# A fused attention and expert kernel on one core: two loads, one group of key turns and ACT's transfers moved in the first pair, and a new order of the ending

## The chip, the cores and the metric

The kernel runs on one core of a Trainium2 chip. Its engines work in parallel, each through its own list of instructions in order, and are held together by semaphores: PE (matrix multiply), DVE (vector), ACT (scalar), POOL (GpSimd) and SP, which here only issues transfers. Transfers run on 16 DMA engines that all queues share. The metric is the device time of one execution in microseconds (us); less is better. The kernel before took 330.53 us, the median of three runs from 329.59 to 330.92.

## The reference, cut to what matters

The input is x of 8 batches of 64 rows by 512, and a context of 8 batches of 1601 rows by 512. Three blocks follow one another, each added to x:

```
x = x + cross(layernorm(x), context)     # scores over 1601 keys, softmax, values
x = x + attn(layernorm(x))               # 16 heads of 32, a sigmoid in place of the softmax, gates
x = x + experts(layernorm(x))            # each row goes to the one of 8 experts with the top logit
# attn:    k, q = l2norm(xn @ Wk), l2norm(xn @ Wq)
#          res = sigmoid((q k^T - 0.295) * 15);  out = ((res * gate_q * gate_k) @ v) @ Wo + bo
# experts: sel = argmax(x @ gate_w.T);  out += (xs @ w_up.T * silu(xs @ w_gate.T)) @ w_down.T
```

The gates are dot products of q and k with the short vectors gq and gk. Everything is 32-bit float.

## The kernel before, in words

**Pairs.** Two batches make a pair of 128 rows (a row per partition), so there are four pairs, numbered 0 to 3 (`_L` is 3, `_B` is 2). Pair 0 is written out, pairs 1 and 2 are a loop, pair 3 is written out again. For each pair PE computes the scores of the pair against its own 1601 keys in 13 units (`score`, lines 1304 to 1348), ACT takes the exponentials, PE turns them (`turn_numerators`) and weighs the context with them (`weigh`), in four chunks of keys. The self attention of pair p - 1 runs between the score units of pair p, as steps with names: "sum", "on", "y" (cross attention's value product), "stats", "norm", "a2" (row statistics, normalization and its turn), "q", "k", "v", "graw", "fold" (products and gates), "kT", "turn" (turned keys and queries), "align0", "align1" (the scores of the heads), "bd" (DVE writes the sigmoid's values in diagonal blocks), "gT", "col" (collapse), "o" (output product), "h", "route", "rank" (top expert and the row's place in the expert's list).

**Keys.** The scores need the keys turned. Part of them PE turns through PSUM (`turn_keys`, lines 1269 to 1277; ACT and DVE move the result, `move_keys`, line 342). The rest is read from the context a second time in a layout that DVE can turn in place: `load_split` (line 364) issues transfers of 512-byte pieces in parts 0 to 3, and `turn_split` (line 868) turns them on DVE into the ring CT_sb. For pair 1 SP issues the lower half of parts 0 and 1, and ACT the upper half, in `upper_first` (line 762), between its copies. Part 2 of pair 1 is issued by SP once DVE has turned part 0 of pair 1.

**Weights in the first pair.** SP's list is in order. From line 439 it reads: attention weights awq and awk, context chunk 1, split part 0 (lower), wv, split part 1 (lower), awv, awo, and then split part 2. POOL waits for awq and awk (lines 565 and 566) and multiplies them, 512 columns at a time, by gq and gk (line 575, eight times). Behind the second multiplication, still in POOL's order, stands `pair_bias(0)`, which copies `ccur`, a bias per row. DVE's `shift(0)` (line 891: the maximum of the scores and this bias) needs `ccur`, and ACT's exponentials need the shift. DVE sums the products of POOL (`gate_sums`, line 1081), two buffers in turn.

**The ending.** Behind pair 3's weighing stands the list `ENDING` (line 88) and then `LATE` (line 93). All engines walk the same two lists, and each picks out its own part of every step. Entries with `_L` are steps of pair 3's self attention, the others steps of the wide expert tiles 0 to 3 (64 rows of each of two experts): "get" (POOL gathers the rows), "xT" (turn), "up0" to "up3" (gate and up products, 4 matmuls each), "act" (ACT's tanh, then two operations of DVE), "hT" (turn), "down" (8 matmuls, and DVE's addition of the result to the rows). The rows that don't fit in the wide tiles go into two narrow tiles 4 and 5, whose rows are known only after pair 3's "rank": DVE makes the choice (`choose(_L)`), PE finds the rows (`find_tokens`), POOL gathers them, and a loop of rounds (one round here) computes them, behind `LATE`. After `ENDING` DVE first counts how many rounds there are (lines 1172 to 1176), then makes the choice, then finds the rows, and then does the first "act" of `LATE`. POOL scatters the finished rows; tiles of `LATE_WIDE` are scattered in the loop of rounds, the others in `ENDING`, and `stored` counts the scatters for the last wait.

## Time and profile before

| | us |
|---|---|
| median of three runs | 330.53 |
| the profiled execution | 324.69 |
| its span, first to last instruction | 323.0 |
| PE busy | 294.6 (91%) |
| DVE busy | 165.2 (51%) |
| ACT busy | 87.9 (27%) |
| POOL busy | 79.4 (25%) |
| mean granted TensorE clock | 0.975 of full |

The profiled execution was shorter than the median of the timed runs. The span ends with the scatter of the last narrow tile, issued at 318.62 us. The chain of work that ended last is of no use here: it holds that scatter alone (0.3% of the span). So the order of time and the idle time in front of instructions have to be read instead. In such a row the columns are: start, duration, engine, line, operation, destination<-source, shape, count, and in brackets the idle time of the engine just before and what ended it. Neighbouring instructions of one kind are merged into one row.

### The profile page before, as it was taken

Reading aid. Unit: us, or ns where it says so; the run is one execution under the profiler, and the core shown is the slowest. Engines: PE = TensorE matmul, PEld = TensorE weight load, DVE = VectorE, ACT = ScalarE, POOL = GpSimd, SP = SyncE. Lnnn points to the kernel's source line nnn. Section 1 sums busy time; section 2 is a strip of 40 time slices with the busy share of each in tenths; the row PEclk is TensorE's granted clock in tenths of the full one; section 3 lists DMA queues with packets and bytes.
Section 4 is the critical chain, followed back from the end, with each engine's and each line's share of the span. In section 5 each row is a group of like instructions: output and inputs, shape, how many; then the busy total and the mean of one; then the engine's idle time right before and its main releaser. Section 6 shows DMA issues by size and latency. Waiting matters only on the chain. (4 is left out here: it accounts for less than half of the span.)

```text
span 323.0 us, 4958 instructions
## 1 busy us (share of the span) xinstructions
PE 294.6 (91%) x1628; PEld 143.3 (44%) x1628; DVE 165.2 (51%) x381; ACT 87.9 (27%) x209; POOL 79.4 (25%) x87
## 2 busy tenths in 40 slices
PE   5899998999679999999999999998998899898992
PEld 4689544633223554333465433455533244442330
DVE  3305382373086767448594638657551434735341
ACT  2133211444001436310264510143411114411210
POOL 5300003328112600022440021262111435103202
PEclk9799998999959999999999999999999999999998
DMA  7999999999996999899999399999215995152300
GB/s 238 375 296 286 231 315 318 289 232 275 227 386 200 213 270 223 168 306 386 234 229 338 81 207 380 309 298 360 90 67 179 422 411 225 42 213 78 143 13 36
DMA packets 67541, 77.41 MB, mean 240 GB/s; under 512 B 3220, under 2 KB 46260, under 8 KB 66497
## 3 DMA queue, kind: packets, MB, share of 16 engines
q1 hardware_dynamic: 60656, 69.76, 76.6%
q0 software_dynamic: 1552, 4.78, 4.2%
q10 hardware_dynamic: 5312, 2.62, 3.7%
q8 instruction: 11, 0.18, 0.2%
q14 instruction: 10, 0.07, 0.1%
HBM read 74.00 MB, written 3.67 MB: 240 GB/s over the span
## 5 line engine op out<-in xcount | busy, mean ns | idle before, releaser
L874 DVE STREAM_TRANSPOSE CT_sb<-FF_sb 128x1024 f32<-128x1024 f32 (+1 forms) x56 | 50.7, 952 | 22.0 <-DMA FF_sb<-ctx 20.8
L1385 PE MATMUL ST<-CTX_sb,PR_sb 128*64 128x512 f32 (+1 forms) x208 | 48.2, 600 | 1.1 <-ACT PR_sb L361 1.1
L1347 PE MATMUL SC<-CT_sb,QC_sb 128*64 128x512 f32 x112 | 29.8, 650 | 4.9 <-DVE CT_sb L874 4.9
L1230 PE MATMUL A<-AW_sb,normT_sb 128*128 128x512 f32 x64 | 29.5, 604 | 0.1
L1385 PEld LDWEIGHTS ST<-CTX_sb,PR_sb 128*64 128x64 f32 (+1 forms) x208 | 13.9, 136 | 23.2 <-issue 22.3
L1230 PEld LDWEIGHTS A<-AW_sb,normT_sb 128*128 128x128 f32 x64 | 11.5, 189 | 15.7 <-issue 11.9
L1253 PE MATMUL A<-AW_sb,WQK_sb 128*128 128x256 f32 x64 | 15.9, 412 | 1.5 <-DMA WQK_sb<-wq 1.5
L546 POOL TENSOR_TENSOR rn_sb<-ss_sb,nhalf_sb 128x16 f32<-128x16 f32 x4 | 11.7, 2917 | 22.3 <-DVE ss_sb L948 22.3
L575 POOL TENSOR_TENSOR sq_sb<-AW_sb,rowv_sb 128x512 f32<-128x512 f32 x4 | 5.1, 1273 | 45.9 <-DMA AW_sb<-awk 35.2
L1347 PEld LDWEIGHTS SC<-CT_sb,QC_sb 128*64 128x64 f32 x112 | 7.3, 144 | 20.2 <-issue 11.0
L1230 PE MATMUL A<-AO_sb,rawT_sb 128*128 128x512 f32 x32 | 14.8, 605 | 1.2 <-DVE rawT_sb L987 1.2
L1327 PE MATMUL SC<-CT_sb,QC_sb 128*64 128x256 f32 x112 | 15.7, 418 | 0.0
L1253 PEld LDWEIGHTS A<-AW_sb,WQK_sb 128*128 128x128 f32 x64 | 13.1, 208 | 3.9 <-DMA WQK_sb<-wq 1.8
L1230 PE MATMUL A<-WV_sb,rawT_sb 128*128 128x512 f32 x32 | 14.7, 602 | 0.0
L693 ACT COPY QC_sb<-QK_sb 32x128 f32 (+1 forms) x48 | 14.2, 296 | 1.1
L1286 PE MATMUL A<-AO_sb,WQK_sb 128*128 128x128 f32 (+1 forms) x64 | 14.5, 382 | 0.0
L714 ACT COPY rawT_sb<-A 128x512 f32<-128x512 f32 x4 | 2.3, 586 | 42.8 <-PE A L1223 34.3
L549 POOL TENSOR_TENSOR rn_sb<-ss_sb,nhalf_sb 128x16 f32<-128x16 f32 x4 | 11.6, 2903 | 6.8 <-DVE ss_sb L955 6.8
L540 POOL TENSOR_TENSOR rstd_sb<-rstd_sb,halves_sb 128x3 f32<-128x3 f32 x4 | 3.5, 877 | 39.2 <-DVE rstd_sb L933 39.2
L558 POOL TENSOR_TENSOR rstd_sb<-rstd_sb,nhalf_sb 128x1 f32<-128x1 f32 x4 | 2.2, 562 | 39.5 <-DVE rstd_sb L995 39.5
L701 ACT ACTIVATE PR_sb<-SC,mx_sb 128x512 f32<-128x512 f32 x12 | 8.1, 684 | 12.9 <-DVE mx_sb L898 12.9
L889 DVE TENSOR_REDUCE mx_sb<-SC 128x1 f32<-128x512 f32 x12 | 8.2, 681 | 6.4 <-PE SC L1327 6.3
(261 smaller groups left out, 482.4 us busy)
## 6 DMA issues: line engine op xcount, KB each, us to landing
CTX_sb<-ctx SPq DMA_DIRECT2D x24, 1024.0 KB, 11.7
FF_sb<-ctx SPq DMA_DIRECT2D x48, 256.0 KB, 6.9
FF_sb<-ctx SPq DMA_DIRECT2D x52, 128.0 KB, 6.1
CTX_sb<-wgu SPq DMA_DIRECT2D x4, 1024.0 KB, 13.0
CTX_sb<-wdn SPq DMA_DIRECT2D x5, 512.0 KB, 16.4
FF_sb<-ctx ACTq DMA_DIRECT2D x8, 256.0 KB, 12.1
FF_sb<-wgu SPq DMA_DIRECT2D x2, 1024.0 KB, 7.6
rows<-XR_sb SPq DMA_DIRECT2D x3, 512.0 KB, 7.3
```

The lines of the kernel that those rows point to most:

```text
L546: g.tensor_tensor(rn[:, 0:HEADS], ss[:, 0:HEADS], nhalf[:, 0:HEADS], ALU.pow).then_inc(s["powq"], 1)
L549: g.tensor_tensor(rn[:, HEADS:], ss[:, HEADS:], nhalf[:, HEADS:], ALU.pow).then_inc(s["powk"], 1)
L693: a.copy(qcurP[m * Q:(m + 1) * Q, j, :], qk[j * Q:(j + 1) * Q, m, bass.ds(p * P, P)]).then_inc(s["qcurP_made"], 1)
L701: a.activation(prow[:, keys], chunk_scores[c], ACT.Exp, bias=mx[:, NCH + 2:NCH + 3], scale=scale, accum_out=esum[:, c:c + 1]).then_inc(s[" ...
L874: v.transpose(ring[:, c, :, to:to + n * Q].rearrange("p k (b r) -> p k b r", r=Q), split[:, :, at:at + n, c * Q:(c + 1) * Q]).then_inc(s[" ...
L889: link(v.tensor_reduce(mx[:, c:c + 1], chunk_scores[c], AX.X, ALU.max))
L1230: last = t_.matmul(bank, left[:, c, :], right[:, c, :], start=(c == 0), stop=(c == DC - 1))
L1253: last = t_.matmul(AB[m % 2][:, 0:2 * P], wq[:, c, m * P:(m + 1) * P], xnT[:, c, 2 * P * half:2 * P * (half + 1)], start=(c == 0), stop=(c ...
L1286: last = t_.matmul(AB[m % 2][:, n], wkT[:, c, m * P:(m + 1) * P], qpT[:, c, n], start=(c == 0), stop=(c == DC - 1))
L1327: last = t_.matmul(SC[q, at:at + GT * P], queries(p, own)[:, i, q], ring[:, i, k, at:at + GT * P], start=(i == 0), stop=(i == DC - 1))
L1347: last = t_.matmul(SC[q, ch * D:(ch + 1) * D], queries(p, own)[:, c, q], ring[:, c, k, :], start=(c == 0), stop=(c == DC - 1))
L1385: last = t_.matmul(ST[q, :], probs[0:w, t, q], ctxb[0:w, k, t, :], start=(t == 0), stop=(t == KT - 1))
```

## The change

It has four parts. In SP's list awq and awk go behind the lower half of split part 0, and wv behind the lower half of part 1. On ACT both `upper_first` go behind the copies of the turned keys, the copy of `crow` comes earlier, and the copy of `call` stands between the two. On DVE the four `turn_split` of pair 1's first keys go in front of the gate sums and of the move of the numerators. The ending gets a new order, with tile 1's act, hT and down in `LATE`; DVE's choice goes in front of the counting of the rounds.

```diff
-ENDING = ((0, "get"), (1, "get"), (_L, "sum"), (0, "xT"), (_L, "on"), (1, "xT"), (_L, "y"), (0, "up0"), (0, "up1"), (0, "up2"), (0, "up3"),
-          (_L, "stats"), (_L, "norm"), (2, "get"), (3, "get"), (_L, "a2"), (1, "up0"), (0, "act"), (_L, "q"), (_L, "graw"), (0, "hT"),
-          (_L, "k"), (_L, "fold"), (_L, "v"), (0, "down"), (2, "xT"), (_L, "kT"), (_L, "turn"), (1, "up1"), (1, "up2"),
-          (_L, "align0"), (_L, "align1"), (1, "up3"), (2, "up0"), (_L, "bd"), (_L, "gT"), (1, "act"), (_L, "col"), (3, "xT"),
-          (_L, "o"), (1, "hT"), (_L, "hnorm"), (_L, "h"), (1, "down"), (_L, "route"), (2, "up1"), (2, "up2"), (_L, "rank"), (2, "up3"))
-LATE = ((2, "act"), (3, "up0"), (3, "up1"), (2, "hT"), (3, "up2"), (3, "up3"), (3, "act"), (2, "down"), (3, "hT"), (3, "down"))
+ENDING = ((0, "get"), (1, "get"), (_L, "sum"), (0, "xT"), (_L, "on"), (_L, "y"), (0, "up0"), (0, "up1"), (0, "up2"), (0, "up3"),
+          (_L, "stats"), (_L, "norm"), (2, "get"), (3, "get"), (_L, "a2"), (0, "act"), (1, "xT"), (_L, "q"), (_L, "graw"), (0, "hT"),
+          (_L, "k"), (_L, "fold"), (_L, "v"), (_L, "kT"), (_L, "turn"), (1, "up0"), (1, "up1"), (_L, "align0"), (_L, "align1"),
+          (0, "down"), (_L, "bd"), (_L, "gT"), (_L, "col"), (2, "xT"), (_L, "o"), (1, "up2"), (_L, "hnorm"), (_L, "h"), (1, "up3"),
+          (_L, "route"), (2, "up0"), (2, "up1"), (_L, "rank"), (2, "up2"))
+LATE = ((1, "act"), (2, "up3"), (1, "hT"), (3, "xT"), (2, "act"), (1, "down"), (3, "up0"), (2, "hT"), (3, "up1"), (3, "up2"),
+        (2, "down"), (3, "up3"), (3, "act"), (3, "hT"), (3, "down"))
-LATE_WIDE = (2, 3)
+LATE_WIDE = (1, 2, 3)
...
             sp.wait_ge(s["qp_made"], 2 * DC)
-            load_weight(awq, "awq", "aq_in")
-            load_weight(awk, "awk", "ak_in")
             load_chunk(0, 1)
             sp.wait_ge(s["keysT_made"], split_turned(0, FIRST.keys(1, 3)))
             load_split(sp, 1, 0, LOWER)
-            load_weight(wv, "wv", "wv_in")
+            load_weight(awq, "awq", "aq_in")
+            load_weight(awk, "awk", "ak_in")
             sp.wait_ge(s["keysT_made"], split_turned(0, FIRST.keys(0, 3)))
             load_split(sp, 1, 1, LOWER)
+            load_weight(wv, "wv", "wv_in")
             load_weight(awv, "awv", "av_in")
...
-            for turn in FIRST.turns[2:6]:
+            for turn in FIRST.turns[2:5]:
+                move_keys(act, a.copy, 0, 0, turn)
+            act.wait_ge(s["c_made"], 1)
+            a.copy(crow, AB[1][:, :]).then_inc(s["c_moved"], 1)
+            for turn in FIRST.turns[5:]:
                 move_keys(act, a.copy, 0, 0, turn)
             upper_first(0, FIRST.keys(1, 3), 0)
-            move_keys(act, a.copy, 0, 0, FIRST.turns[6])
-            act.wait_ge(s["c_made"], 1)
-            a.copy(crow, AB[1][:, :]).then_inc(s["c_moved"], 1)
-            upper_first(0, FIRST.keys(0, 3), 1)
             act.wait_ge(s["c_made"], 2)
             a.copy(call[:], AB[1][:, 0:PAIRS + E]).then_inc(s["c_moved"], 1)
+            upper_first(0, FIRST.keys(0, 3), 1)
             exponentials(0)
...
-            gate_sums(0, 2)
-            move_numerators(dve, v.tensor_copy, 0, 1)
             for c in range(DC):
                 turn_split(1, 1, c)
-            gate_sums(2, 4)
+            move_numerators(dve, v.tensor_copy, 0, 1)
+            gate_sums(0, 4)
             move_numerators(dve, v.tensor_copy, 0, 3)
...
+            dve.wait_ge(s["slot_made"], PAIRS)
+            choose(_L)
             link(v.tensor_tensor(cnt[:, 2:2 + E], A1[:, E:2 * E], filled[:], ALU.add))
...
             v.tensor_scalar(rounds[0:1, 0:1], cnt[0:1, 1:2], 1.0, None, ALU.add).then_inc(s["rounds_made"], 1)
...
-            dve.wait_ge(s["slot_made"], PAIRS)
-            choose(_L)
             dve.wait_ge(s["tok_made"], 1)
             find_rows(link)
```

## Rows read from the trace of the kernel before

**Rows 1.** The page: PE's busy time, and the DMA share in 40 slices.

```profile
PE 294.6 (91%) x1628; PEld 143.3 (44%) x1628; DVE 165.2 (51%) x381; ACT 87.9 (27%) x209; POOL 79.4 (25%) x87
DMA  7999999999996999899999399999215995152300
```

**Rows 2.** Windows: stretch, length, busy by engine, then PEclk, DMA share, GB/s.

```profile
48.00:50.00 2.00, 2.00 (x14) 1.23 (x16) 0.71 (x1) 0.00 (x0) 0.42 (x1) 1.00 1.05 397
52.00:54.00 2.00, 1.61 (x14) 1.09 (x14) 0.00 (x0) 0.82 (x2) 0.07 (x1) 1.00 1.10 320
78.00:84.00 6.00, 6.00 (x23) 2.25 (x20) 0.00 (x0) 1.09 (x2) 4.06 (x4) 1.00 1.23 216
54.00:58.00 4.00, 4.00 (x23) 2.66 (x24) 0.00 (x0) 0.00 (x0) 0.00 (x0) 0.57 1.21 254
```

**Rows 3.** DMA issues: the load of awk, with KB and us to landing.

```profile
AW_sb<-awk SPq DMA_DIRECT2D x1, 1024.0 KB, 9.6
```

**Rows 4.** Order of time, the first pair, from gates to first weighing.

```profile
49.58 1.27 POOL L575 TENSOR_TENSOR sq_sb<-AW_sb,rowv_sb 128x512 f32<-128x512 f32 x1 [35.20 <-DMA AW_sb<-awk]
...
52.39 1.08 PE L1327 MATMUL SC<-CT_sb,QK_sb 128*64 128x256 f32 x8 [1.53 <-ACT CT_sb L351]
...
59.93 0.69 ACT L701 ACTIVATE PR_sb<-SC,mx_sb 128x512 f32<-128x512 f32 x1 [1.70 <-DVE mx_sb L898]
...
62.22 0.49 ACT L681 COPY QK_sb<-A 128x384 f32<-128x384 f32 x1
...
64.49 0.59 ACT L361 COPY PR_sb<-TR 128x512 f32<-128x512 f32 x1
...
65.13 3.65 PE L1385 MATMUL ST<-CTX_sb,PR_sb 128*64 128x512 f32 x16 [0.24 <-ACT PR_sb L361]
```

**Rows 5.** Order of time: part 2 of pair 1 issued, and waited for.

```profile
70.25 12.51 SPq L370 DMA_DIRECT2D FF_sb<-ctx  x8
...
89.21 3.50 DVE L874 STREAM_TRANSPOSE CT_sb<-FF_sb 128x1024 f32<-128x1024 f32 x3 [11.51 <-DMA FF_sb<-ctx]
90.51 5.15 PE L1347 MATMUL SC<-CT_sb,QC_sb 128*64 128x512 f32 x12 [4.90 <-DVE CT_sb L874]
...
96.28 0.66 PE L1223 MATMUL A<-ident_sb,a_sb 128*128 128x128 f32 x4 [0.62 <-DVE a_sb L936]
```

**Rows 6.** Windows: the ending, from the last weighing to the narrow tiles.

```profile
245.64:303.26 57.62, 52.40 (x264) 22.74 (x265) 26.35 (x69) 13.02 (x27) 16.95 (x13) 1.00 0.58 224
```

**Rows 7.** Order of time, the ending, around "a2" and "q".

```profile
256.95 2.67 DVE L943 TENSOR_SCALAR normT_sb<-rawT_sb,vec_sb 128x128 f32<-128x128 f32 x4 [1.30 <-ACT rawT_sb L714]
257.63 1.08 PE L1589 MATMUL SC<-CTX_sb,QK_sb 128*64 128x512 f32 x4 [1.34 <-DMA CTX_sb<-wdn]
```

**Rows 8.** Order of time, the ending, from tile 0's "down" to "col".

```profile
270.09 1.94 PE L1610 MATMUL SC<-FF_sb,QK_sb 128*64 128x512 f32 x8
...
272.07 0.69 DVE L1159 TENSOR_TENSOR CT_sb<-SC,CT_sb 128x512 f32<-128x512 f32 x1 [3.52 <-PE SC L1610]
...
275.70 1.95 PE L1437 MATMUL A<-WQK_sb,rawT_sb 128*64 128x256 f32 x16 [0.34 <-issue]
...
278.30 1.78 DVE L981 TENSOR_SCALAR WQK_sb<-res_sb 64x512 f32<-64x512 f32 x4
...
280.14 1.08 PE L1452 MATMUL A<-WQK_sb,vs_sb 128*32 128x128 f32 x32 [0.19 <-DVE WQK_sb L981]
```

**Rows 9.** Order of time, behind "rank", and around tile 3's last "up".

```profile
293.23 0.16 DVE L1172 TENSOR_TENSOR cnt_sb<-A,filled_sb 128x8 f32<-128x8 f32 x1
...
294.54 0.20 PE L1564 MATMUL A<-token_sb,CT_sb 128*128 128x1 f16 x2 [0.96 <-DVE CT_sb L1036]
...
295.52 0.42 DVE L1155 SCALAR_TENSOR_TENSOR QK_sb<-QK_sb,TR 128x256 f32<-128x256 f32 x1
...
298.25 0.59 PE L1589 MATMUL SC<-WV_sb,QK_sb 128*64 128x512 f32 x1
...
299.76 0.42 DVE L1155 SCALAR_TENSOR_TENSOR QK_sb<-QK_sb,SC 128x256 f32<-128x256 f32 x1
```

More of the change, by code:

```diff
@@ L262, in x_bank, with stored @@
             return A1 if f == NT - 1 else TR[0]
-        def stored(r):
-            return 16 * ((NW - len(LATE_WIDE)) // 2 + (len(LATE_WIDE) + NN) // 2 * (r + 1))
+        def stored(i, r):
+            wide = sum(f % 2 == i for f in range(NW) if f not in LATE_WIDE)
+            late = sum(f % 2 == i for f in LATE_WIDE + tuple(range(NW, NT)))
+            return 16 * (wide + late * (r + 1))
         def tile_number(f, r):
@@ L646, in _ @@
                 for i in range(2):
-                    pool.wait_ge(s_stored[i], stored(r))
+                    pool.wait_ge(s_stored[i], stored(i, r))
                 settle(pool)
@@ L1171, in _, with find_rows @@
             link, n = linker("round_chain", 0)
+            def find_rows(link):
+                link(v.tensor_reduce(tok[:, 2, :], token_bank.rearrange("p (i f) -> p f i", i=PAIRS), AX.X, ALU.add))
+                v.tensor_scalar(idxg[:], tok[:, 2, :], -1.0, 0.0, ALU.add, ALU.max).then_inc(s["idxg_made"], 1)
+            dve.wait_ge(s["slot_made"], PAIRS)
+            choose(_L)
             link(v.tensor_tensor(cnt[:, 2:2 + E], A1[:, E:2 * E], filled[:], ALU.add))
@@ L1176, in _ @@
             v.tensor_scalar(rounds[0:1, 0:1], cnt[0:1, 1:2], 1.0, None, ALU.add).then_inc(s["rounds_made"], 1)
-            def find_rows(link):
-                link(v.tensor_reduce(tok[:, 2, :], token_bank.rearrange("p (i f) -> p f i", i=PAIRS), AX.X, ALU.add))
-                v.tensor_scalar(idxg[:], tok[:, 2, :], -1.0, 0.0, ALU.add, ALU.max).then_inc(s["idxg_made"], 1)
-            dve.wait_ge(s["slot_made"], PAIRS)
-            choose(_L)
             dve.wait_ge(s["tok_made"], 1)
@@ L1210, in _ @@
                 for i in range(2):
-                    dve.wait_ge(s_stored[i], stored(r))
+                    dve.wait_ge(s_stored[i], stored(i, r))
                 assert n[0] == ROUND_LINKS
```

## The prediction

> **What bounds the kernel now.** I read the page first. PE is busy for 294.6 us of the 323.0, and the DMA share is at 9 tenths without a break over the first slices, then it loosens [rows 1]. So PE's stream sets the time wherever it has work, and the first hundred microseconds are the place where transfers could set it. The chain that ended last shows only the last scatter, so I went through PE's idle times in order of time. There are two kinds of them. In the start PE waits 1.53 us for an ACT copy at 52.39 [rows 4], and 4.90 us ahead of 90.51 for keys that DVE could not turn, because DVE itself waited 11.51 us for split part 2 of pair 1 [rows 5]. That second wait ends with a transfer. In the ending, from 245.64 to 303.26, PE is busy 52.40 of 57.62 us, which leaves 5.2 us of idle time in some nine pieces [rows 6]. PE does the same matmuls after the change, so it can win at most these pieces, and it loses what new ones open.
>
> **The start: where the first shift goes.** The windows give the DMA's speeds: pieces of 2 KB alone go at 397 GB/s, pieces of 512 bytes from one queue at 216, 2 KB from SP beside 512 bytes from ACT at 320, and 512 bytes from both at 254 [rows 2]. In SP's list chunk 1 (2.1 MB) now has the place of awq and awk (2.1 MB), so it lands when awk did: POOL's first gate product, released by awk, starts at 49.58, and awk took 9.6 us from its issue [rows 3, 4]. Then comes the lower half of part 0, 1.05 MB at 216 GB/s: 4.9 us, to 54.3. ACT's upper half is now issued only from about 50 us. Then awq and awk, 2.1 MB, beside ACT's small pieces. If the DMA engines take turns piece by piece, SP gets four fifths of 320 GB/s, or 256: 8.2 us, and awk lands at 62.5. The bounds: with nothing beside it 2.1 MB take 5.3 us (59.6); with all of ACT's 1.05 MB ahead of it at 216 GB/s 67.3. I take 62.5, since the 320 GB/s were measured with both kinds in flight.
>
> The Trainium skill ("DMA: Bandwidth & Descriptors", section "Queues, rings and completion order") says that each DMA engine takes turns between the queues at the grain of a packet of several descriptors. With packets of like counts that is my piece-by-piece share; with ACT's packets shorter, awk would land up to 3 us sooner.
>
> POOL's order is gates 0 and 1 and then the copy of `ccur`, and DVE's shift needs `ccur`. So the shift, which waited for ACT's copy of `call` before, now waits for awk: two products of 1.27 us [rows 4] and three or four short instructions of some 0.2 us each (the like of 0.16 in rows 9), 0.7 us. The exponentials start at 62.5 + 2.5 + 0.7 = 65.7 instead of 59.93. ACT then goes on as before: 2.3 us to its copy at 62.22, two such copies of 0.49, and the numerators' copy of 0.59 [rows 4]. In the old order these lay under PE's products of queries; now they are behind each other, and the first weighing starts at 65.7 + 2.3 + 1.0 + 0.6 = 69.6 instead of 65.13, 4.5 us late. ACT's issues behind its copies do remove the 1.53 us at 52.39, and the half clock behind it (granted clock 0.57 from 54 to 58 [rows 2]), but PE only reaches the numerators sooner, at about 61, and waits there longer. After such a wait it runs at the low clock of 1.2 GHz for some microseconds: behind the 4.90 us of rows 5, 12 matmuls took 5.15 us where four take 1.08 at 2.4 GHz [rows 7], 1.9 us too much. I take 2.4 for the longer wait. PE is 6.9 us late when it comes to pair 1's scores.
>
> What covers this: PE waited 4.90 us there anyway, the 1.9 us of low clock go with that wait, and another 0.62 us of idle time stands ahead of 96.28 [rows 5]. Together 7.4 us, so 6.9 us cost nothing, with 0.5 us to spare. If awk lands at 67.3, 4.8 us later, 4.3 us are left over.
>
> **The start: pair 1's keys.** DVE turns them right behind the shift: 4 turns of about 1.2 us (three took 3.50 [rows 5]). From 66.1 they end near 70.9, about where they ended before (SP issued part 2 at 70.25, which waits for them [rows 5]). So this move wins nothing: the transfer they wait for and the late shift hold them. Nor would an earlier issue help, for the same bytes stand ahead of part 2 in the queues and the DMA is never idle there. DVE's move of numerators 1 is now behind the turns, at 71.6; PE needs it behind the first weighing, at 69.6 + 3.65 + the low clock, later than 75. The gate sums come later too (end near 83, before the pair's sum needs DVE at about 84), and POOL's clearing and added row end near 88, ahead of the 92 us at which DVE wants them. These cost nothing with some microseconds of cover; on the low side they can't gain, since part 2 holds everything.
>
> Part 2's landing itself may move. Some 1000 more of ACT's small pieces now run beside 2 KB pieces rather than beside other small ones. At 320 against 397 GB/s such a piece costs 2.8 ns, at 254 against 216 it costs 1.7 ns: 1.2 us more in all. Bounds -1 (the order could as well spare the slow passage from small to large pieces) to +1.2; I take +0.8. All that comes later in pair 1 shifts by it.
>
> **The ending.** I walked PE's new list with the durations of before (product 3.5, "up" 0.87, "down" 1.87, turn 0.5 from start to start).
> - Behind "on" PE has no xT of tile 1 left to do: idle +0.3. Tile 1's "up0" no longer stands ahead of "q", so the 1.34 us wait for tile 1's weights goes [rows 7]. In its place PE waits for normT: 0.7 us until its first quarter is there, and 0.9 us because DVE's four operations take 2.67 us [rows 7] beside POOL's gathers and addition. Together +0.3.
> - From "align0" DVE's order is: two scalings, then **tile 0's addition**, then "bd". The addition waits for "down" of tile 0, which PE does behind "align1". Before: "align" at 275.70, "bd" at 278.30, "col" at 280.14 [rows 8]. Now, counted from "align0": "down" starts at +1.75, its result is added from +1.75 + 1.98 = +3.7 (270.09 to 272.07 [rows 8]) for 0.69, "bd" runs from +4.4 for 1.78, and "col" can start at +6.25. PE's fill is "down" 1.87 and "gT" 0.5, which end at +4.15. A hole of 2.1 us instead of 0.19. Without the addition in front "bd" would end at +4.45.
> - The waits of 0.34 [rows 8] and of about 0.6 ahead of "h" go, and that ahead of "o" shrinks by 0.2, since other steps fill them: -1.1.
> - The choice in front of the counting: about 0.9 us of DVE's counting (from 293.23 to PE's 294.54, less the choice itself and the signal) leave the way to PE's wait of 0.96 us [rows 9]. With less fill ahead, 0.4 us are left: -0.6.
> - Tile 1's "act" now stands on DVE behind choice, counting and finding, 2.4 us in all (293.23 to 295.94 less the wait inside [rows 9]). PE has 0.15 + 0.87 us to do meanwhile: a hole of 1.1 us ahead of "hT" of tile 1.
> - At the end of `LATE` "down" of tile 2 stood between tile 3's last "up" and its "hT". Now it stands ahead of that "up", and nothing is between. From the last matmul of "up" (298.25) to the end of "act" on DVE (300.18) it takes 1.93 us [rows 9], of which 0.45 is the matmul's own pace: a hole of 1.5 us.
>
> The pieces sum to 0.3 + 0.3 + 1.9 - 1.1 - 0.6 + 1.1 + 1.5 = +3.4. Walking the starts instead I reach the narrow tiles at 305.9 against 303.26, +2.6, since a few changes of kind between steps disappear. I take +2.7. The narrow rows are gathered some 3 us sooner, but PE had no idle time left ahead of 303.26, so that hides nothing new. Bounds: -1.9 if neither hole of DVE's order opens, +3.4 if all do.
>
> On normT: the Trainium skill ("SBUF — State Buffer", section "Who interferes with whom") says that VectorE in its two-port mode and GpSimd lock each other out for whole instructions. The 2.67 us agree. If POOL's addition fell clear of the four operations in the new order, 0.9 us of the hole at "q" would go and the sum be 0.9 lower; POOL's steps shift with DVE's, so I leave it.
>
> **The sum.** The profiled execution took 324.69 us (span 323.0 and 1.7 around it). 324.69 + 0 + 0.8 + 2.7 = 328.2. The median of the timed runs was 330.53, 5.8 us above the profiled one; I take the same difference of 3.5 us there: 334.0.
>
> **Rivals.**
> *The ending's new order pays (faster).* The mechanism is in the ending: the waits on tile 1's weights (1.34), on the choice (0.6 of 0.96) and of the short ones (1.1) go, and the two holes of DVE's order and the last "hT" don't open, because PE reaches "down" of tile 0 or tile 3's "up" late enough. Then it is -1.9, with part 2 at +0.2: 328.8. It decides if the hole ahead of "col" stays under 0.3 us and that ahead of tile 3's "hT" under 0.5. For it: the old list has real waits there. Against: the old list had a "down" as fill in the last place, the new one has nothing.
> *awk lands late, beyond the cover (slower still).* Should ACT's transfers take more of the DMA, 4 us come on top: 338. Against: the share of 320 GB/s measured with both in flight.
> *They cancel.* Only one of the DVE holes opens, or part 2 lands 1 us sooner: 331.5, no change that can be told.
> That the change doesn't do what it says is in the forecast itself: the first keys are turned no earlier, as the shift comes later.
>
> **Chances.** A measurement of this kernel tells a change from none at about 0.5%, 1.65 us. Forecast 0.53, awk late 0.12, cancelled 0.17, faster 0.18. So slower 0.65, same 0.17, faster 0.18. The range goes from 328.8 (the first rival; half of its chance lies below) to 337.8, near the second; the forecast's own is 332 to 336.
>
> **What would show it.** POOL's first line 575 row near 62.6, and the first exponential near 65.7; PE idle there for some 4 to 5 us; no idle piece over 1 us ahead of the scores of pair 1 near 90; the PE row of line 1452 ("col") behind a wait of 2 us for line 981; a wait of 1.5 us ahead of tile 3's "hT". I am wrong if `ccur` is there before 60 us, or if the ending's idle sum is under 5 us.

## The result, and the profile after

The changed kernel took 334.24 us (median of four runs, 331.1 to 335.0), the kernel before 330.06 beside it. The ratio, here and below, is taken over the fast runs alone and so needn't be that of the medians: 1.032, 95% interval 1.020 to 1.044. In a second comparison, with 30 runs of before and 7 of the changed kernel, the medians were 328.91 and 332.42, ratio 1.011 (1.003 to 1.019). Both say slower, by 1 and by 3%; the size can't be had closer, since the kernel before, measured against itself, gave a ratio of 1.021 (below). The forecast was 334.0, +3.5 us, ratio 1.0106.

The changed kernel's page: the same work on PE, DVE, ACT and POOL as in [rows 1], but a span of 332.2 us, 9.2 more. PEclk, the granted clock in tenths of full, drops in slices 8 to 10, in and behind the long wait of the start, and once more in slice 35, in the ending.

```profile
PE 294.8 (89%) x1628; PEld 143.7 (43%) x1628; DVE 165.3 (50%) x381; ACT 87.5 (26%) x209; POOL 79.4 (24%) x87
PEclk9999999757999999999999999999999999799997
DMA  6999999999996998899999699999026992524000
```

Its order of time at the start. This answers [rows 4] and [rows 5]: awk ends the wait at 67.07, where 62.6 was forecast; POOL needs two products and the copy of `ccur`; the first exponential follows at 70.22, not 65.7; PE waits 12.30 us for it. Part 2 is issued at 75.10 and DVE starts on its last pieces at 92.32.

```profile
67.07 1.26 POOL L578 TENSOR_TENSOR sq_sb<-AW_sb,rowv_sb 128x512 f32<-128x512 f32 x1 [52.89 <-DMA AW_sb<-awk]
68.29 1.25 POOL L578 TENSOR_TENSOR kh_sb<-AW_sb,rowv_sb 128x512 f32<-128x512 f32 x1
69.49 0.18 POOL L532 COPY ccur_sb<-call_sb 128x1 f32<-128x1 f32 x1
...
70.22 0.69 ACT L704 ACTIVATE PR_sb<-SC,mx_sb 128x512 f32<-128x512 f32 x1 [18.97 <-DVE mx_sb L902]
70.38 4.62 DVE L878 STREAM_TRANSPOSE CT_sb<-FF_sb 128x1024 f32<-128x1024 f32 x4
71.05 1.97 PE L1359 MATMUL TR<-ident_sb,PR_sb 128*128 128x128 f32 x8 [12.30 <-ACT PR_sb L704]
...
75.10 10.08 SPq L373 DMA_DIRECT2D FF_sb<-ctx  x8
...
92.32 3.50 DVE L878 STREAM_TRANSPOSE CT_sb<-FF_sb 128x1024 f32<-128x1024 f32 x3 [3.12 <-DMA FF_sb<-ctx]
...
99.84 0.66 PE L1226 MATMUL A<-ident_sb,a_sb 128*128 128x128 f32 x4
```

PE's wait of 4.90 us in [rows 5] is gone, and still the a2 turn of pair 0 comes at 99.84 instead of 96.28. In the chain of waits (start, length, what) this stretch is now awk, the exponentials, then PE's work up to the product "y" at 92.48 and DVE's steps behind it; the wait for part 2 isn't in it. The waits for the next pairs' split parts are.

```profile
51.08 15.83 DMA AW_sb<-awk
70.22 2.41 ACT PR_sb L704 x8
73.93 6.37 PE ST L1388 x16
...
92.48 3.65 PE A L1233 x8
...
138.38 8.07 DMA FF_sb<-ctx
...
192.28 8.04 DMA FF_sb<-ctx
```

The ending, in the order of time. Against [rows 7]: "q" waits twice for DVE's quarters of normT. Against [rows 8]: "col" (line 1455) waits 1.89 us, since DVE adds tile 0 first (line 1162, 281.53) and then makes the four products. Against [rows 9]: the wait on the choice is 0.17, and two new waits of 0.86 and 1.49 stand ahead of the hT of tiles 1 and 3.

```profile
262.44 2.66 DVE L947 TENSOR_SCALAR normT_sb<-rawT_sb,vec_sb 128x128 f32<-128x128 f32 x4 [1.30 <-ACT rawT_sb L717]
262.84 1.12 PE L1233 MATMUL A<-AW_sb,normT_sb 128*128 128x512 f32 x2 [0.62 <-DVE normT_sb L947]
...
264.64 1.55 PE L1233 MATMUL A<-AW_sb,normT_sb 128*128 128x512 f32 x3 [0.68 <-DVE normT_sb L947]
...
281.53 0.69 DVE L1162 TENSOR_TENSOR CT_sb<-SC,CT_sb 128x512 f32<-128x512 f32 x1 [1.02 <-PE SC L1613]
282.14 1.77 DVE L985 TENSOR_SCALAR WQK_sb<-res_sb 64x512 f32<-64x512 f32 x4
283.96 1.73 PE L1455 MATMUL A<-WQK_sb,vs_sb 128*32 128x128 f32 x32 [1.89 <-DVE WQK_sb L985]
...
297.68 0.20 PE L1567 MATMUL A<-token_sb,CT_sb 128*128 128x1 f16 x2 [0.17 <-DVE CT_sb L1040]
...
299.74 0.41 PE L1601 MATMUL ST<-ident_sb,QK_sb 128*128 128x128 f32 x2 [0.86 <-DVE QK_sb L1158]
...
309.71 0.41 PE L1601 MATMUL ST<-ident_sb,QK_sb 128*128 128x128 f32 x2 [1.49 <-DVE QK_sb L1158]
```

The 9.19 us between the two traces lie in three places, counted from one instruction to its counterpart: 3.56 up to pair 0's a2 turn (96.28 to 99.84), 2.26 from there to the last weighing product (148.77 against 151.03), where not a line is changed, and 3.37 in the ending (58.70 to 62.07). The tail is equal. So one comparison of two traces puts a quarter of the loss into untouched code, and this is what the experiments had to explain.

### The profile page after: what moved, and what is told of

Same layout as the page of the kernel before. It is cut to its first block, busy times and chain, and to the rows that moved or that the text cites. A ratio compares the mean times of both kernels' runs of the same rounds, so it can differ in the third digit from the quotient of the medians.

```text
span 332.2 us, 4959 instructions
## 1 busy us (share of the span) xinstructions
PE 294.8 (89%) x1628; PEld 143.7 (43%) x1628; DVE 165.3 (50%) x381; ACT 87.5 (26%) x209; POOL 79.4 (24%) x87
## 4 chain that ended last, share of the span: by engine, by line
PE 60%; DVE 13%; DMA 12%; SPq 5%; issue 4%; ACT 3%; POOL 1%; DVEq 0%; POOLq 0%; ACTq 0%
PE A L1233 15%; PE ST L1388 8%; DVE CT_sb L878 5%; DMA FF_sb<-ctx 5%; DMA AW_sb<-awk 5%; PE A L1256 4%; SPq L373 4%; PE SC L1330 4%; PE SC L1592 3%; PE SC L1613 3%; PE TR L1233 3%; PE A L1289 3%; PE A L1226 3%; PE A L1440 2%; DMA WQK_sb<-wq 2%
## 5 line engine op out<-in xcount | busy, mean ns | idle before, releaser
L1388 PE MATMUL ST<-CTX_sb,PR_sb 128*64 128x512 f32 (+1 forms) x208 | 50.9, 628 | 1.8 <-ACT PR_sb L364 1.8
L1350 PE MATMUL SC<-CT_sb,QC_sb 128*64 128x512 f32 x112 | 27.2, 603 | 0.0
L1388 PEld LDWEIGHTS ST<-CTX_sb,PR_sb 128*64 128x64 f32 (+1 forms) x208 | 14.6, 143 | 26.0 <-issue 24.3
L578 POOL TENSOR_TENSOR sq_sb<-AW_sb,rowv_sb 128x512 f32<-128x512 f32 x4 | 5.1, 1265 | 64.0 <-DMA AW_sb<-awk 52.9
L1359 PE MATMUL TR<-ident_sb,PR_sb 128*128 128x128 f32 (+1 forms) x52 | 9.0, 304 | 12.3 <-ACT PR_sb L704 12.3
L1359 PEld LDWEIGHTS TR<-ident_sb,PR_sb 128*128 128x128 f32 (+1 forms) x52 | 6.6, 153 | 20.2 <-ACT PR_sb L704 13.6
L1256 PE MATMUL A<-AW_sb,WQK_sb 128*128 128x256 f32 x64 | 14.2, 381 | 1.1 <-DMA WQK_sb<-wq 1.1
L1330 PE MATMUL SC<-CT_sb,QC_sb 128*64 128x256 f32 x112 | 14.3, 388 | 0.0
L1256 PEld LDWEIGHTS A<-AW_sb,WQK_sb 128*128 128x128 f32 x64 | 12.0, 190 | 2.9 <-DMA WQK_sb<-wq 1.4
```

Of the source, the lines that this page charges most:

```text
L1256: last = t_.matmul(AB[m % 2][:, 0:2 * P], wq[:, c, m * P:(m + 1) * P], xnT[:, c, 2 * P * half:2 * P * (half + 1)], start=(c == 0), stop=(c ...
L1330: last = t_.matmul(SC[q, at:at + GT * P], queries(p, own)[:, i, q], ring[:, i, k, at:at + GT * P], start=(i == 0), stop=(i == DC - 1))
L1350: last = t_.matmul(SC[q, ch * D:(ch + 1) * D], queries(p, own)[:, c, q], ring[:, c, k, :], start=(c == 0), stop=(c == DC - 1))
L1359: last = t_.transpose(TR[c % 2][0:w, (t - lo) * P:(t - lo + 1) * P], prow[:, t * P:t * P + w], ident[:, :])
L1388: last = t_.matmul(ST[q, :], probs[0:w, t, q], ctxb[0:w, k, t, :], start=(t == 0), stop=(t == KT - 1))
```

## The experiments

**What one trace is worth: the kernel before, again.**

> The kernel before, unchanged, profiled and timed once more, to see what a second execution of the same program differs by. Theory A (all of the 9.2 us between the two profiles is the change): part 2 of pair 1 lands near 89.1 again, its 256 KB pieces 1.25 us apart, and the span is 323 +- 1. Theory B (some 2 to 3 us of the 9.2 us are the DMA's speed in that execution, since the pieces of part 2 came 1.33 us apart in the changed kernel's profile and the loop of pairs lost 0.9 us per pair there): the pieces come 1.3 to 1.35 us apart in some executions of this kernel too, and the span is 325 to 328.

Six runs had the median 334.83 (330.5 to 336.4), beside 328.47 over eleven runs of the same program (325.9 to 336.9): a ratio of 1.021 (1.015 to 1.027) between a kernel and itself. Five of the six lie within 2 us (334.5 to 336.4), which doesn't look like independent draws from the wide spread. The intervals take them as independent and are then too narrow: here a ratio up to some 1.02 proves nothing by itself. In its order of time the a2 turn comes at 99.27, where the changed kernel has 99.84.

```profile
92.19 3.50 DVE L874 STREAM_TRANSPOSE CT_sb<-FF_sb 128x1024 f32<-128x1024 f32 x3 [13.32 <-DMA FF_sb<-ctx]
...
93.50 4.53 PE L1347 MATMUL SC<-CT_sb,QC_sb 128*64 128x512 f32 x12 [5.86 <-DVE CT_sb L874]
...
99.27 0.65 PE L1223 MATMUL A<-ident_sb,a_sb 128*128 128x128 f32 x4 [1.24 <-DVE a_sb L936]
```

So the rival that puts the difference into the spread between executions holds here: DVE's last turns of part 2 come 3 us later than in [rows 5], and the a2 turn with them, in an unchanged kernel. The first profile of before was one of its fastest executions.

**The change in halves: its start alone, twice, and its ending alone.** start_only is the changed kernel with the old lists and the old place of the choice; ending_only is the reverse.

```diff
 # start_only, start_again: the changed kernel with
-ENDING, LATE, LATE_WIDE = the new ones;   choose(_L) ahead of the counting
+ENDING, LATE, LATE_WIDE = the old ones;   choose(_L) behind the counting
 # ending_only: the kernel before with the new ones
```

> The changed kernel with the ending of before (both lists, the late tiles, and choice behind counting). If the parts add up, PE waits some 10 to 12 us for the first exponential, the a2 turn of pair 0 is 3 to 3.6 us later than before, and the whole is +1 to +3.5 us against before (1.003 to 1.011). By my forecast's sum the start costs 0.8 us (1.002).

> The kernel before with the new ending alone. Forecast of the mechanism: a hole of 1.9 to 2.1 us ahead of col and 1.5 us ahead of the last hT of the wide tiles, the way from the last weighing to the narrow tiles is 60.5 to 61 us instead of 57.6, the whole +2.7 to +3.8 us (1.008 to 1.0115). The rival, that the removed waits pay for the holes, says -1.9 to +0.5 us.

> The changed start with the ending of before, as start_only, once more, for its second trace and its median. Theory 1 (the late shift is a bound of its own): pair 0's a2 turn comes 32 to 33 us behind the landing of awk and more than 7.2 us behind that of part 2; the wait for awk costs 0.4 to 3 us, the more the faster part 2 lands, so the median is 1 to 2 us above that of before, ratio 1.004, and the lowest runs of before (322) are not reached. Rival (the cover of 7.4 us holds, and only part 2 counts): a2 exactly 7.2 us behind part 2, ratio 1.00 and the same lowest runs.

start_only: 331.39 us (325.3 to 338.4), ratio 1.000 (0.992 to 1.008). start_again: 329.38 over twelve runs (322.8 to 336.4) beside 328.14 (322.5 to 335.3), no interval. ending_only: 330.89, ratio 1.008 (1.002 to 1.014). Beside the 1.021 of a kernel against itself no time here tells one of the halves from nothing; both have to be measured in the order of time. For the start: in start_only DVE has the last pieces at 90.13, 2 us sooner than in the second trace of before, and the a2 turn comes no sooner:

```profile
70.61 1.97 PE L1358 MATMUL TR<-ident_sb,PR_sb 128*128 128x128 f32 x8 [9.42 <-ACT PR_sb L703]
...
90.13 3.50 DVE L877 STREAM_TRANSPOSE CT_sb<-FF_sb 128x1024 f32<-128x1024 f32 x3 [1.36 <-DMA FF_sb<-ctx]
...
99.41 0.66 PE L1225 MATMUL A<-ident_sb,a_sb 128*128 128x128 f32 x4
```

From DVE's first of these turns to the a2 turn it takes 7.07 or 7.08 us in all eleven traces whose first shift doesn't wait for awk, whatever their total. In the four with the changed start it takes 7.52, 9.28, 7.92 and 7.59 (after, start_only, after_again, start_again), and there the a2 turn comes 32.9, 32.9, 32.3 and 33.1 us behind the landing of awk. So there are two bounds, part 2 and the late shift, and in the changed kernel the second is the later one, by 0.4 to 2.2 us, mean 1.0. The rival in start_again, that part 2 alone counts, is refuted by the trace (7.59 and not 7.07); its other half, that the lowest runs stay as low, came true (322.8 and 322.5). In time the start's cost of about 1 us is below what the runs tell.

**The late shift taken away.**

```diff
+            pair_bias(0)
             pool.wait_ge(s["rowv_in"], 16)
             pool.wait_ge(s["aq_in"], 16)
...
-                if n == 2:
-                    pair_bias(0)
```

> The changed kernel with POOL's copy of ccur in front of its waits for awq and awk, so that the first shift does not hang on awk. Theory 1 (the bias behind awk is what costs at the start): PE's 12.3 us wait for the first exponential goes, and the a2 turn of pair 0 comes 3 us earlier, so the whole is 3 us (0.991) faster than the changed kernel. Theory 2 (the landing of part 2 of pair 1 sets it, and it is late because the DMA moved the same bytes more slowly): the 12.3 us wait goes too, but PE waits 8 to 10 us for the keys near 92 instead, and the a2 turn of pair 0 gains under 0.7 us.

336.05 us, one of six runs far out (750.5), no ratio. The order of time shows the exchange: the exponentials start at 62.48 although awk landed only at 70.4, and the 12.30 us of PE's wait become 2.96 there and 5.83 for part 2. Part 2 was slow in this execution, and a2 comes at 102.03, not sooner. DVE's turn of pair 1's first keys, which the change put right behind the shift, starts only at 68.86, behind a wait of 12.36 us for their transfer.

```profile
62.48 0.69 ACT L703 ACTIVATE PR_sb<-SC,mx_sb 128x512 f32<-128x512 f32 x1 [9.62 <-issue]
...
94.96 3.50 DVE L877 STREAM_TRANSPOSE CT_sb<-FF_sb 128x1024 f32<-128x1024 f32 x3 [11.81 <-DMA FF_sb<-ctx]
...
96.26 4.81 PE L1349 MATMUL SC<-CT_sb,QC_sb 128*64 128x512 f32 x12 [5.83 <-DVE CT_sb L877]
...
102.03 0.66 PE L1225 MATMUL A<-ident_sb,a_sb 128*128 128x128 f32 x4 [0.97 <-DVE a_sb L939]
```

**What part 2's landing is worth, in both directions.** In weights_late awv and awo are issued behind it, in more_bytes two more transfers of 1 MB stand ahead of it (their copies are read by nobody).

```diff
 # weights_late
-            load_weight(awv, "awv", "av_in")
-            sp.wait_ge(s["qk_made"], 2 * DC)
-            sp.wait_ge(s["c_made"], 2)
-            load_weight(awo, "awo", "awo_in")
             split_after(1, NEXT.keys(1, 3), 1, 2)
+            (the same four lines)
 # more_bytes
             load_weight(awv, "awv", "av_in")
+            for i in range(2):
+                sp.dma_start(spare[i], A["awk"]).then_inc(s["spare_in"], 16)
```

> The kernel before, with one thing moved on SP: the two weights of the second attention's values and output (awv, awo, 1 MB each as they lie in memory) are issued behind the second split part of pair 1 instead of ahead of it. Theory 1 (the landing of that part sets pair 0's a2 turn, whatever the start does, and it is set by the bytes queued ahead of it): part 2 lands 4 to 6 us earlier (before: 92.1 in the second profile of that kernel, so about 87), the wait of 5.9 us that PE has for it shrinks to under 2 us, pair 0's a2 turn comes at 95 to 96 instead of 99.3 (or at 93 where the pace of the pieces is the fast one), the last weighing and the end come as much earlier, 3 to 4 us, ratio 0.990. Theory 2 (the part is late because it is issued late and its pieces have their own pace of 1.3 us each): it lands at the same time, ratio 1.00. Theory 3 (the two weights then arrive too late for v and o of pair 0): the wait only moves to there, ratio 1.00 with a wait on L1419's awv or on awo.

> The kernel before with two more 1 MB transfers on SP's queue behind awv, from the memory of the chip to a place in it that nothing reads, so two weights' bytes more stand ahead of the second split part of pair 1; nothing else is changed, and no engine waits for them. Theory 1 (what stands in the stream ahead of that part sets pair 0's a2 turn, and a later turn is carried to the end): the part lands about 5 us later (97 instead of 92), the wait of PE for it grows by as much, pair 0's a2 turn comes at 104 to 105 instead of 99 to 100, and the run is 4 to 5 us longer, ratio 1.013. Taken with the run in which two weights were moved behind the part (a2 turn at 93.9, the end where it was), it says whether the start counts in one direction only. Rival (the stream has slack later, so the periods of pairs 1 to 3 take the 5 us back): the a2 turn is as late, but the last weighing comes under 2 us later, ratio 1.005 or less.

more_bytes: 334.64 us beside 328.0, ratio 1.030 (1.019 to 1.041). The a2 turn is at 104.17, 4.9 later than in before_again, and the last one at 265.91 against 261.33 there: next to that trace nothing is given back, and the rival with its slack falls. Of the 6.6 us between the medians (more than the 4 to 5 expected) this explains 4.6 to 4.9. The size rests on single traces: over the six with the old start and the old bytes the a2 turn lies between 96.28 and 102.89 and the last one between 255.63 and 264.91. The direction rests on more: both turns of more_bytes lie behind all of them, and from the issue of part 2 (70.70) to DVE's first turn of it takes 26.4 us, against 19.0 to 22.3 in those six.

```profile
97.09 3.50 DVE L877 STREAM_TRANSPOSE CT_sb<-FF_sb 128x1024 f32<-128x1024 f32 x3 [19.91 <-DMA FF_sb<-ctx]
...
98.39 4.37 PE L1350 MATMUL SC<-CT_sb,QC_sb 128*64 128x512 f32 x12 [14.03 <-DVE CT_sb L877]
...
104.17 0.66 PE L1226 MATMUL A<-ident_sb,a_sb 128*128 128x128 f32 x4 [1.41 <-DVE a_sb L939]
```

weights_late: 328.43 beside 328.91, ratio 1.002 (0.995 to 1.009). The a2 turn is at 93.92, 5.4 earlier than in before_again, more than expected, but the 3 to 4 us expected at the end didn't come: DVE waits 4.02 us for part 3 until 111.09, PE waits 3.82 behind it, and the a2 turn of pair 1 comes at 153.51, where before_again has 153.72.

```profile
86.85 3.50 DVE L874 STREAM_TRANSPOSE CT_sb<-FF_sb 128x1024 f32<-128x1024 f32 x3 [6.38 <-DMA FF_sb<-ctx]
...
93.92 0.65 PE L1223 MATMUL A<-ident_sb,a_sb 128*128 128x128 f32 x4 [2.11 <-DVE a_sb L936]
...
111.09 2.49 DVE L874 STREAM_TRANSPOSE CT_sb<-FF_sb 128x512 f32<-128x512 f32 x4 [4.02 <-DMA FF_sb<-ctx]
...
115.13 2.96 PE L1437 MATMUL A<-WQK_sb,rawT_sb 128*64 128x256 f32 x16 [3.82 <-issue]
```

The stretch from pair 0's a2 turn to pair 1's says it without regard to an execution's pace: 59.6, 61.2 and 60.4 us in the three traces with the two weights late (weights_late, choose_late_w, turn_first; the last two below), 52.9 to 54.5 in the twelve others. So bytes put ahead of part 2 are carried to the end. Moving bytes behind it pays only until the next part, which has the same bytes ahead of it as ever.

**The changed kernel again.**

> The changed kernel with nothing altered, in the same call. If runs of one program differ by up to 2 per cent from execution to execution through the pace of the first 90 us of transfers, as the kernel before did (325.9 to 336.9 over eleven runs), this one comes out at 331 to 337, and its ratio to the kernel before lies between 1.00 and 1.02, not at 1.032 again. Its profile should have the stretch from the last weighing to the last tile's turn at 61 to 62 us and the holes ahead of col (1.9) and of tile 3's hT (1.5), whatever its total; pair 0's a2 turn may lie anywhere from 96 to 100.

332.42 us over seven runs beside 328.91 over thirty: ratio 1.011 (1.003 to 1.019). Time and ratio were as expected, the holes and the stretch too (1.89, 1.49, 60.9). Only the a2 turn, 101.40, lies above the 96 to 100 expected.

**The ending's holes closed one after the other**, on the kernel before with the new ending.

```diff
 # end_col: tile 0's down behind col
-          (0, "down"), (_L, "bd"), (_L, "gT"), (_L, "col"), (2, "xT"), ...
+          (_L, "bd"), (_L, "gT"), (_L, "col"), (0, "down"), (2, "xT"), ...
 # end_both: end_col, and in LATE
-        (2, "down"), (3, "up3"), (3, "act"), (3, "hT"), (3, "down"))
+        (3, "up3"), (3, "act"), (2, "down"), (3, "hT"), (3, "down"))
```

> The kernel before with the new ending (as ending_only), but tile 0's down step is put behind col instead of ahead of bd, so that DVE's addition of that tile (0.69 us) no longer stands ahead of the four block-diagonal products that col waits for. Theory 1 (the hole of 1.9 us ahead of col is that addition with its wait for PE's product, and the clock falls behind the hole): the hole shrinks to under 1.2 us, o runs in 3.7 instead of 4.2 us, and the stretch from the last weighing's last product to the last tile's turn (58.6 in the kernel before, 60.9 in ending_only, 62.1 in after) is 1.0 to 1.6 us shorter than in ending_only: 59.5 to 60. Rival (col waits for the gate mask or for vp, not for the four products): the hole stays and the stretch stays at 60.9.

> As end_col, and in the late part tile 2's down step moves from ahead of tile 3's up3 to between tile 3's activation and its hT, so that 0.9 us of PE's work lies where PE stood for 1.49 us. Theory 1: that hole falls to 0.6 us or less, the stretch is another 0.9 us shorter than in end_col, about 58.8, which is what the kernel before has (58.6): the new order is then worth nothing once its holes are closed. Rival: the activation of tile 3 is now late behind up3, so the hole of 0.86 ahead of tile 1's hT and the one at tile 3 only change places: stretch as in end_col, 59.5 to 60.

Medians 330.60 and 330.61 beside 328.91, ratios 1.003 (0.996 to 1.009) and 1.003 (0.997 to 1.009). The windows from pair 3's a2 turn to the turn of the last narrow tile tell more (length, PE busy, PEclk, DMA share, GB/s). The kernel before, first trace; its second one has 48.22:

```profile
255.63:303.75 48.12, 44.08 (x232) 1.00 0.53 205
```

The changed kernel, first and second trace (ending_only has 50.63, at full clock too):

```profile
261.13:312.94 51.81, 46.07 (x236) 0.97 0.50 195
```

```profile
263.74:314.35 50.61, 44.65 (x236) 1.00 0.52 203
```

end_col and end_both:

```profile
260.91:312.84 51.93, 46.24 (x236) 0.97 0.50 196
```

```profile
262.85:311.62 48.77, 44.53 (x236) 1.00 0.53 205
```

At the full clock the new ending takes 50.6 us and the old one 48.2 in this window: +2.4. Of it 1.9 are idle time (50.6 less 44.7 against 48.1 less 44.1), and 0.5 are the four matmuls of tile 1's "xT" (x236 against x232), which stood ahead of the a2 turn in the old order. From the last weighing on, with them in both, it is 60.9 against 58.6 and 58.7: +2.2. end_both brings the window to 48.77 and the whole stretch to 59.0, 0.3 to 0.5 above the old order and 0.8 to 0.9 above the old order with the same early choice (58.1 and 58.2, below). Neither kernel's time differs from before beyond the interval.

Its two edits together are worth 1.9, and the waits say which of them: nearly all is the second. In end_col the wait ahead of "col" is 0.98 instead of 1.90, but a new one of 0.89 stands ahead of "gT", where "down" had been PE's fill; end_both has 0.99 and 0.88. Their sum is what the one hole was. "col" comes 1.7 us sooner, counted from "align0" (4.4 instead of 6.1), and then PE has "down" still to do, which takes as long. Only a wait of 0.23 ahead of "o" went with it. The second edit took the whole 1.49 us ahead of tile 3's hT away.

```profile
280.43 0.63 PE L1226 MATMUL A<-ident_sb,kh_sb 128*128 128x128 f32 x4 [0.89 <-DVE res_sb L973]
282.05 1.75 PE L1455 MATMUL A<-WQK_sb,vs_sb 128*32 128x128 f32 x32 [0.98 <-DVE WQK_sb L984]
```

**The best part alone, and two candidates.** choose_early is the kernel before with the choice ahead of the count; choose_late_w adds weights_late; turn_first is the changed start with the bias first, the weights late, and the old order with the choice early.

> The kernel before with one small part of the ending's change alone: DVE makes the last pair's choice and the lookup of rows ahead of the five small instructions that count the rounds, as the changed kernel does; the order of steps stays as before. Theory: the wait of 0.96 us that PE has for DVE's pick ahead of the lookup product falls to 0.2 us, as in the changed kernel, and nothing is late behind it, so the stretch from the last pair's a2 turn to the last tile's turn, 48.1 to 48.2 at full clock in three traces, becomes 47.4, ratio 0.998. Rival: tile 2's product fills PE behind it anyway, the count of rounds is late for the tail, and the stretch stays at 48.2.

> choose_early with the two weights issued behind the second split part of pair 1, as in weights_late, as the candidate for a version faster than both kernels. If the two edits are independent: pair 0's a2 turn at 94, the last stretch at 47.4, and the run 0.5 to 1.3 us shorter than the kernel before, ratio 0.997; what the earlier a2 turn brings is expected to be lost again in pair 1, where the next split part comes when it came before (111 us).

> The changed kernel's start with its two obstacles taken away, and the ending of before with the choice ahead of the count: POOL makes the bias column before its waits for awq and awk, and awv and awo are issued behind the second split part of pair 1. Theory 1 (two things end pair 0's a2 turn: 7.2 us behind the landing of part 2, in eight traces, or 32.9 us behind the landing of awk where the first shift waits for it): the shift no longer waits for awk, so the first exponential is at 60 to 62 and a2 comes 7.2 us behind part 2, which lands at 85 to 88, so at 92 to 95, with the last stretch 47.4 at full clock. Theory 2 (turning pair 1's first keys right behind the shift wins by itself once the shift is early): part 2 is issued 2 us sooner than the 70.25 of before and lands as much sooner than in weights_late (86.7), the a2 turn is at 92 or earlier. Either way pair 1 gives the gain back, as in weights_late: 327 to 328, ratio 0.997 to 1.00.

choose_early: 328.37 beside 328.0, ratio 1.005 (0.998 to 1.012). The wait fell from the 0.96 of [rows 9] to 0.18:

```profile
301.06 0.20 PE L1564 MATMUL A<-token_sb,CT_sb 128*128 128x1 f16 x2 [0.18 <-DVE CT_sb L1036]
```

Its window had the low clock (49.58), so the 47.4 expected can't be read there; choose_late_w and turn_first, with the same ending at full clock, have 47.34 and 47.5 instead of 48.2. choose_late_w:

```profile
258.41:305.75 47.34, 44.12 (x232) 1.00 0.54 208
```

It took 327.14 us beside 328.0, ratio 1.006 (0.998 to 1.015): not told from the kernel before, and the lowest median of all runs. turn_first: 331.1 beside 328.14, ratio 1.012 (1.004 to 1.019), not the 0.997 to 1.00 expected. Its first exponential was at 64.1, its a2 turn at 95.71, 7.1 behind DVE's first turn of part 2 (88.64), and the turn of pair 1 at 156.15, 2.6 us later than in weights_late, behind a wait of 5.54 us at 117.06. The stretch between the two turns, 60.4 us, is that of the other two kernels with the weights late. But it doesn't test an earlier turn of the first keys, for they were not turned earlier: their transfer landed late, DVE waited 11.37 us for it, and part 2 was issued at 74.34 instead of 70.25.

```profile
69.61 4.62 DVE L876 STREAM_TRANSPOSE CT_sb<-FF_sb 128x1024 f32<-128x1024 f32 x4 [11.37 <-DMA FF_sb<-ctx]
```

## Why the prediction was right or wrong, point by point

- **The sum** was +0 for the late shift, +0.8 for part 2, +2.7 for the ending, 3.5 in all, ratio 1.0106. The larger comparison has 3.5 us and 1.011, the first one 4.2 us between the medians and a ratio of 1.032. The direction was right, the size right by the one and three times too small by the other. What the traces show of the change is +1.0 for the late shift, nothing that can be told for part 2 and +2.2 for the ending, 3.2 in all; no step of the kernel accounts for the rest of the 1.032, and a ratio of 1.021 came up without any change. That the sum agrees with the larger comparison is partly luck: the 0.8 for part 2, which can't be seen, fills in for the late shift, which was put at nothing.
- **The step that failed is "so 6.9 us cost nothing, with 0.5 us to spare"**, and under it the term for awk, "awk lands at 62.5". It landed at 66.9. PE came 11.5 us late to pair 1's scores (89.00 against 77.48) where 6.9 was forecast, and nearly the whole of the 4.6 is awk, for the rest of the path held: 3.3 us from the landing to the exponentials (3.2 forecast) and 2.7 us of low clock behind them (2.4 forecast). Within the term it is "the lower half of part 0, 1.05 MB at 216 GB/s: 4.9 us, to 54.3" that failed. The trace's records of the single packets, summed by queue, show SP's 512-byte pieces from 47.1 to 57.0 us: some 150 GB/s before ACT's pieces came at 51.1, and then, from 54 to 57 us, 25 GB/s for SP beside 170 for ACT. The working had let ACT's pieces slow awk alone and not part 0 ahead of it. Not one of the 2 KB pieces of awq and awk moved before 57. Behind 58 they had 254 GB/s beside 55 for ACT, the four fifths and the 256 of the working. In the windows of the changed kernel (PE, PEld, DVE, ACT, POOL, then PEclk, DMA share, GB/s):

```profile
54.00:57.00 3.00, 3.00 (x11) 1.74 (x10) 0.16 (x1) 0.00 (x0) 0.00 (x0) 1.00 1.24 198
57.00:66.00 9.00, 1.75 (x6) 0.73 (x4) 0.00 (x0) 0.00 (x0) 0.00 (x0) 0.80 1.10 297
```

  The landing is near the upper bound of the working, 67.3, but by chance: that bound counts ACT's 1.05 MB ahead of awk (4.9 us) and beside it as well (8.2 us for awq and awk instead of 5.3), and by the working's own rates "all of ACT's ahead" gives 64.5. The rule quoted from the Trainium skill ("DMA: Bandwidth & Descriptors", section "Queues, rings and completion order"), turns between the queues, agrees with this trace behind 58 us, where SP has its four fifths, and not from 54 to 57, where SP's pieces of the same size got 25 GB/s against 170; the measurement decides. The other five traces with ACT's transfers in the new place have such a stretch too, of 2 to 4 us, with SP at 3 to 70 GB/s. Why SP's queue all but stood still there is not shown.
- **The second rival's price was wrong too.** Its condition (awk at 67.3) was all but met, and it asked 4.3 us. The traces show 0.4 to 2.2 for the late shift, mean 1.0. The cover had been counted against the fastest of the traces: in the other five with the old start and the old bytes part 2 landed at 92.1 to 95.7, and there the two bounds lie close together.
- **Part 2's landing, +0.8 in bounds of -1 to +1.2**, was +3.1 between the first two traces. But two traces of before differ by 3.0 themselves, and the four traces with the changed start (90.0 to 93.4) lie within those with the old one (89.1 to 95.7). An effect of the change can't be seen; the bounds lacked the spread from execution to execution.
- **Pair 1's first keys.** "This move wins nothing: the transfer they wait for and the late shift hold them" was right in both parts: with the late shift taken away, DVE still waited for the transfer until 68.86 (after_bias_first) and 69.61 (turn_first), later than the 65.53 of the kernel before.
- **The ending** was sized at +2.7 for the stretch from the last weighing on. It measured +2.2 at the full clock (60.9 against 58.6 and 58.7) and +3.4 in the profiled execution. Hole by hole: ahead of "col" 2.1 forecast, 1.89 measured; ahead of tile 1's hT 1.1 and 0.86; ahead of tile 3's hT 1.5 and 1.49; at "q" 0.7 and 0.9 against 0.62 and 0.68; on the choice 0.4 and 0.17. The wait for tile 1's weights went. The other 1.2 us are PE at the low clock behind the hole ahead of "col". That isn't shown to be a price of the new order: the same dip hit six of fifteen traces, among them start_only, more_bytes and choose_early with the old order (50.04, 49.92 and 49.58 where 48.2, 48.2 and 47.4 are had without it), while after_again and ending_only had the same hole and no dip.
- **normT.** The hole at "q" stayed, so the case that the Trainium skill's "SBUF — State Buffer", section "Who interferes with whom", opened, a shorter one if POOL fell clear of the four operations, did not occur in pair 3. It does occur in the same trace in pairs 0 to 2, where POOL's addition ends before they begin: there they take 1.11 us and not 2.66.

```profile
101.15 1.11 DVE L947 TENSOR_SCALAR normT_sb<-rawT_sb,vec_sb 128x128 f32<-128x128 f32 x4 [1.30 <-ACT rawT_sb L717]
...
263.22 1.27 POOL L546 TENSOR_TENSOR x_sb<-x_sb,rowv_sb 128x512 f32<-128x512 f32 x1
```

  In pair 3 one of the four took 1.89 us instead of 0.34 and ended 0.1 us behind POOL's addition. That agrees with this section of the Trainium skill, and the price is 1.55 us on DVE, more than the 0.9 of the working; of it PE's second wait at "q", 0.68, might go; no run shows that.
- **The base.** The forecast added its sum to 324.69 and lifted it by 5.8 to the median, as if a profiled execution stood in a fixed relation to the others. With this kernel it doesn't; the right base was the median alone.
- **The rival that the ending pays** fell: both DVE holes and the last one opened, each near its forecast.

## What to carry to other kernels

Before a difference between two traces is explained, look at how much of it lies in code that the change does not touch: here a quarter, and the same program gave 322 to 337 us. If a kernel against itself can give 1.02, an interval around 1.01 is no proof. Where two waits end within a few microseconds of each other, write each as an event plus a constant (here part 2 plus 7.2, awk plus 33) and compare the constants over all traces, for that separates them when the totals can't. Where all transfers stand in one ordered stream, moving bytes behind one consumer pays only up to the next one, while bytes added in front were carried to the end. And before a hole is closed by moving the work that fills the engine, count what that work leaves open: one hole of 1.9 us became two of 0.9.

## What the runs showed of the hardware that was not expected

- The kernel before, one program on one core, took between 321.7 and 336.9 us over 81 runs in four comparisons.
- Two queues with 512-byte pieces did not always share alike. In the kernel before, from 57 to 61 us, SP's and ACT's had 144 GB/s each; in the changed kernel, from 54 to 57, SP's had 25 and ACT's 170 (198 in all). Behind that, with 2 KB pieces on SP's queue the bytes went some four to one (254 and 55).
- One VectorE operation of 0.34 us took 1.89 beside a GpSimd addition of 1.27 us, in pair 3 of five traces (before, before_again, after, after_again, end_both) and never in their pairs 0 to 2.
- PE's granted clock was at half, 1.2 GHz, for one stretch of 3.4 us in six of fifteen endings and at full in the nine others; the traces with one and without it had the same holes ahead. It cost 1.2 to 1.9 us where a like trace without it is at hand. Where it lies differs: 2.8 to 3.1 us behind the a2 turn in the three with the old order, from the start of "col" on in the three with the new one. Four of the nine others had such a stretch in pair 3's weighing (221 to 231 us). In start_only, with the old ending, the stretch right behind the a2 turn (length, PE busy, PEclk, DMA share, GB/s) was this one; in the same stretch before_again had 1.00. What decides it, no run showed.

```profile
260.52:268.86 8.34, 6.72 (x16) 0.80 1.01 415
```
